# Two expert stages rewritten in a chain of sixteen layers: choice in one pass, gathering in units, combination on 32-column parts

## The reference

```python
def _L3_ffn_ref(x, Wc, bc, W1, b1, W2, b2):
    DM, NEXPERTS, SETS, ESIZE = (128, 32, 4, 32)
    grouped = x.reshape(b, s // g, g, d)                       # g = 32 tokens
    logits = jnp.einsum('bntd,des->bntes', grouped, Wc) + bc
    tie = jnp.linspace(0.0, 1e-06, g, dtype=x.dtype).reshape(-1, 1, 1)
    logits = logits + tie
    perm = (logits == jnp.max(logits, axis=-3, keepdims=True)).astype(x.dtype)
    permuted = jnp.einsum('bntd,bntes->bnesd', grouped, perm)
    inner = jax.nn.relu(jnp.einsum('bnesd,esdf->bnesf', permuted, W1) + b1)
    result_permuted = jnp.einsum('bnesf,esdf->bnesd', inner, W2) + b2
    result = jnp.einsum('bnesd,bntes->bntd', result_permuted, perm)
    return result.reshape(b, s, d)
...
x = x + _L3_ffn_ref(_layernorm(x, axis=-1), ...)
```

## Time and profile before

| | before |
|---|---|
| time, median of 2 runs | 2715.27 us (2713.83 to 2716.72) |
| the profiled execution's own time | 2716.01 us |
| its span, first to last instruction | 2714.2 us |
| mean granted TensorE clock | 0.894 |
| TensorE busy | 2225.2 us (82%) |
| VectorE busy | 1772.0 us (65%) |
| ScalarE busy | 1385.8 us (51%) |
| first expert stage | 2302.0 to 2398.6 us |
| second expert stage | 2607.9 to 2705.6 us |

### The profile page before, as it was taken

One profiled execution on the slowest core, in us unless ns is written; L12 is line 12 of the kernel. 1 busy time (PEld: TensorE's weight loads), 2 busy tenths in 40 slices (PEclk: granted clock), 3 DMA queues, 4 the chain that ended last, 5 costly groups with the idle time before them and its releaser, 6 DMA issues. The chain is left out here.

```text
span 2714.2 us, 42839 instructions
## 1 busy us (share of the span) xinstructions
PE 2225.2 (82%) x15196; PEld 1524.2 (56%) x15196; DVE 1772.0 (65%) x4423; ACT 1385.8 (51%) x3630; POOL 718.8 (26%) x472
## 2 busy tenths in 40 slices
PE   6999979889887987978447887768776988689978
PEld 4888846636643653653347774433424765556648
DVE  6777748759746965964656663356456997637863
ACT  3555537738734764864411226563636764326750
POOL 0000016516502642630033420000012976051000
PEclk9999999989988989999678898888987999778986
DMA  1000021100002101001012320000001221100010
GB/s 56 14 19 15 7 72 22 23 20 21 21 5 75 25 17 24 21 16 48 0 36 58 74 46 0 12 12 6 4 12 56 86 70 60 45 10 2 2 65 17
DMA packets 79043, 80.92 MB, mean 30 GB/s; under 512 B 28624, under 2 KB 63952, under 8 KB 77808
## 3 DMA queue, kind: packets, MB, share of 16 engines
q1 hardware_dynamic: 78832, 78.19, 10.1%
HBM read 53.94 MB, written 8.52 MB: 23 GB/s over the span
## 5 line engine op out<-in xcount | busy, mean ns | idle before, releaser
L1014 ACT ACTIVATE window_s<-window_s,window_soft 128x128 f32<-128x128 f32 x512 | 197.7, 394 | 5.0 <-DVE window_soft L1177 5.0
L1084 POOL TENSOR_TENSOR window_s<-window_s,window_soft 128x512 f32<-128x512 f32 x128 | 133.2, 1041 | 218.5 <-DVE window_soft L1114 218.4
L1092 POOL TENSOR_TENSOR window_pa<-window_pa,window_pb 128x1024 f32<-128x1024 f32 x64 | 151.5, 2368 | 148.8 <-DVE window_pb L1159 148.8
L1177 DVE CUSTOM_DVE_ANT_0 window_s<-ps,window_mask,window_nrn 128x128 f32<-128x128 f32 x512 | 148.7, 346 | 46.7 <-PE ps L859 29.9
L3127 DVE TENSOR_TENSOR_SCAN mamba_bx<-ps,mamba_ab 128x256 f32<-128x256 f32 x256 | 154.5, 667 | 18.9 <-PE ps L2913 18.9
L822 PE MATMUL ps<-window_wa,window_sh 128*128 128x512 f32 x256 | 131.3, 638 | 41.4 <-DVE window_pb L1159 28.4
L3297 ACT ACTIVATE rope_p<-ps,rope_mx 128x128 f32<-128x128 f32 (+1 forms) x256 | 104.3, 419 | 53.1 <-DVE rope_mx L3351 53.1
L2910 PE MATMUL ps<-mamba_m,mamba_xt 128*128 128x129 f32 x512 | 102.9, 283 | 29.6 <-ACT mamba_m L2985 20.6
L83 PE MATMUL ps<-x,consts 128*128 128x512 f32 x120 | 77.0, 801 | 46.1 <-PEq L53 40.5
L3015 POOL TENSOR_TENSOR h<-mamba_bx,mamba_cbr 128x1024 f32<-128x1024 f32 x32 | 89.3, 2796 | 93.2 <-DVE mamba_bx L3127 92.7
L2910 PEld LDWEIGHTS ps<-mamba_m,mamba_xt 128*128 128x128 f32 x512 | 82.3, 197 | 49.1 <-issue 49.1
(11 more groups left out here) (607 smaller groups left out, 6235.9 us busy)
## 6 DMA issues: line engine op xcount, KB each, us to landing
mamba_cbr<-mamba_c SPq DMA_DIRECT2D x32, 512.0 KB, 3.7
window_vs<-window_vt SPq DMA_DIRECT2D x64, 128.0 KB, 2.3
delta_xi<-delta_x SPq DMA_DIRECT2D x16, 512.0 KB, 5.1
switch_w<-in_switch_w SPq DMA_DIRECT2D x4, 2048.0 KB, 10.1
window_wa<-in_window_wa SPq DMA_DIRECT2D x4, 1152.0 KB, 6.8
linattn_wb<-in_linattn_wb SPq DMA_DIRECT2D x6, 513.0 KB, 3.5
window_wb<-in_window_wb SPq DMA_DIRECT2D x4, 537.5 KB, 7.7
window_sh<-y SPq DMA_DIRECT2D x16, 128.0 KB, 2.2
```

The lines of the kernel that those rows point to most:

```text
L1014: a = nc.scalar.activation(s[:, k % 2, e, c, :], s[:, k % 2, e, c, :], ACT.Exp, scale=-1.0, bias=soft[:, k % 2, e, 1, c:c + 1], accum_out= ...
L1084: nc.gpsimd.tensor_tensor(s[:, k % 2, e], s[:, k % 2, e], soft[:, k % 2, e, 3, :].unsqueeze(2).to_broadcast([P, QC, P]), ALU.mult)\
L1092: nc.gpsimd.tensor_tensor(own, own, pb[:, :, :, :].rearrange("p a h d -> p (a h d)"), ALU.add)\
L1177: v = nc.vector.tensor_tensor_reduce(s[:, k % 2, e, c, :], K.ps[:, B_S + e, toks(c, P)], mask[:, k % 2, :], nrn[:, k % 4, h:h + 1], 3e38, ...
```

## The change

Only `switch_stage` changes, in five places.

1. Choice in one pass: VectorE adds bias and tie term in one scalar_tensor_tensor straight from PSUM, in place of ScalarE's pass and VectorE's add.
2. Order: the logits of a block and the turning of its tokens alternate on TensorE. The turning of `perm` and the gathering start as soon as two blocks are chosen. VectorE copies a first gathered half block before it makes the fourth choice. ScalarE makes all copies of turned `perm`.
3. Gathering in units: a unit (j, u) is eight matmuls, for the four tiles of block j and for two of the four groups. The groups go to banks j and j + 4; ScalarE copies the one, VectorE the other, and neither waits for the other's copy. `z` is laid out as [feature, group, expert], so the copies write runs of 128 elements, and the first product reads its 64 moving elements 128 elements (512 bytes) apart.
4. The results are turned without b2; copies alternate between ScalarE and VectorE. b2 comes in through matmuls of `perm` (as stationary operand, 128 experts by 128 tokens) with b2.
5. Combination: for each group `perm`'s 32 columns are the stationary operand and `resm[:, group, :]` the moving one, with the output on 32 partitions, so four groups go to four 32-column parts of the array. The sum has tokens on the partitions; ScalarE copies it to `y_tm`, TensorE turns it back, and VectorE adds it to `x`.

```diff
-    z = st.sb("z", [P, ES, NG])
+    z = st.sb("z", [P, NG, ES])
...
+    units = [(0, 0), (1, 0), (0, 1), (2, 0), (1, 1), (3, 0), (2, 1), (3, 1)]
+    seen = {u: n + 1 for n, u in enumerate(units)}
+
+    def picked_to(j, g):
+        return z[:, :, :].rearrange("p (j t g) e -> p j g t e", j=NJ, g=4)[:, j, g]
...
+            def turn_chosen(j):
                 pe.wait_ge(st.chosen, j + 1)
+                pe.wait_ge(st.x_copied, j + 1)
                 for t in range(TPW):
                     mm = nc.tensor.transpose(K.ps[:, j, toks(t, P)], perm[:, toks(TPW * j + t, P)], K.ident)
                 mm.then_inc(st.chosen_tm, 1)
...
+            def pick(j, u):
+                pe.wait_ge(st.chosen_copied, j + 1)
+                if u:
+                    pe.wait_ge(st.picked_act, seen[j, 0])
+                    pe.wait_ge(st.picked_dve, seen[j, 0])
+                for t in range(TPW):
+                    for e in range(2):
+                        g = 2 * u + e
+                        rows, tile = slice(32 * g, 32 * g + 32), toks(TPW * j + t, P)
+                        mm = nc.tensor.matmul(K.ps[:, j + 4 * e, toks(t, P)], h_tm[rows, tile], perm_tm[rows, tile],
+                                              start=True, stop=True)
+                mm.then_inc(st.picked, 1)
...
+            def combine(j):
+                bank = K.ps[:, 4 + j % 2, :]
                 if j >= 2:
+                    pe.wait_ge(st.y_copied, j - 1)
+                for t in range(TPW):
+                    nc.tensor.matmul(bank[:, toks(t, P)], perm[:, toks(TPW * j + t, P)], b2, start=(t == 0), stop=False,
+                                     skip_group_check=True)
+                pe.wait_ge(st.moved_act, 2 * (j + 1))
+                pe.wait_ge(st.moved_dve, 2 * (j + 1))
                 for t in range(TPW):
                     for g in range(4):
+                        n = 4 * (TPW * j + t) + g
+                        mm = nc.tensor.matmul(K.ps[32 * g:32 * g + 32, 4 + j % 2, toks(t, P)], perm[:, toks(n, GT)],
+                                              resm[:, n, :], start=False, stop=True, skip_group_check=True)
+                mm.then_inc(st.y_ready, 1)
...
                     mm = nc.tensor.matmul(K.ps[32 * r:32 * r + 32, q // 8, toks(q % 8, NG)], w1[:, 4 * q + r, :],
-                                          z[:, 4 * q + r, :], start=True, stop=True)
+                                          z[:, :, 4 * q + r], start=True, stop=True)
...
-                nc.scalar.activation(logit[:, toks(j)], K.ps[:, j, :], ACT.Identity, bias=bc).then_inc(st.biased, 1)
...
+                nc.vector.scalar_tensor_tensor(grouped(logit[:, toks(j)]), grouped(K.ps[:, 4 + j, :]), bc,
+                                               tie.unsqueeze(1).to_broadcast([P, 16, GT]), ALU.add, ALU.add)\
+                    .then_inc(st.logits, 1)
...
+            choose(0)
+            choose(1)
+            choose(2)
+            picked(*units[0])
+            choose(3)
+            for j, u in units[1:]:
+                picked(j, u)
```

More of the change, by code:

```diff
@@ L3472, in _, with turn_back @@
+            def turn_back(j):
+                pe.wait_ge(st.y_copied, j + 1)
+                if j >= 2:
+                    pe.wait_ge(st.x_done, j - 1)
+                for t in range(TPW):
+                    mm = nc.tensor.transpose(K.ps[:, 6 + j % 2, toks(t, P)], y_tm[:, toks(TPW * j + t, P)], K.ident)
+                mm.then_inc(st.y_turned, 1)
             outer.pe(pe, 0, K.x, lambda j: None)
@@ L3474, in _ @@
             for j in range(NJ):
[L3475 to L3497, removed]
+                logits(j)
+                turn_x(j)
+            turn_chosen(0)
+            turn_chosen(1)
+            for n, (j, u) in enumerate(units):
+                pick(j, u)
+                if n in (1, 3):
+                    turn_chosen(2 + n // 2)
             pe.wait_ge(st.w2_ready, 32)
-            pe.wait_ge(st.picked_copied, NT)
+            pe.wait_ge(st.picked_act, 8)
+            pe.wait_ge(st.picked_dve, 8)
             for q in range(NQ):
@@ L3516, in _ @@
                             mm.then_inc(st.h2_ready, 1)
[L3517 to L3524, removed]
-            for j in range(NJ):
-                pe.wait_ge(st.result_ready, min(4 * j + 4 + 8, NT))
-                for g in range(16 * j, 16 * j + 16):
-                    mm = nc.tensor.matmul(K.ps[:, 4 + j, toks(g % 16, GT)], resm[:, g, :], perm[:, toks(g, GT)],
-                                          start=True, stop=True)
-                mm.then_inc(st.y_ready, 1)
+            turn_result(0)
@@ L3544, in _ @@
-            for n in range(0, NT, 2):
-                picked_copy(scalar_copy, act, n)
-            for n in range(0, ES // 8, 2):
-                result_copy(scalar_copy, act, n)
+                nc.scalar.activation(h_tm[:, toks(j)], K.ps[:, j, :], ACT.Copy).then_inc(st.x_copied, 1)
+            turned_chosen(0)
+            turned_chosen(1)
+            for n, (j, u) in enumerate(units):
+                picked(j, u)
+                if n in (1, 3):
+                    turned_chosen(2 + n // 2)
@@ new lines, in _ @@
+            for n in range(0, ES // 8, 2):
+                act.wait_ge(st.h2_ready, n + 1)
+                if n:
+                    act.wait_ge(st.h2_copied, n)
+                nc.scalar.activation(result_to(n), K.ps[:, (4 + n) % 8, :].rearrange("p (q g) -> p q g", g=NG), ACT.Copy)\
+                    .then_inc(st.h2_copied, 1)
+            moved(0)
+            moved(2)
+            for j in range(NJ):
+                if j + 1 < NJ:
+                    moved(4 * j + 4)
+                    moved(4 * j + 6)
+                result(j)
```

132 lines of the change are left out of this document (80 added, 52 removed).

## The result

The changed kernel takes 2669.27 us (median of 2 runs, 2667.62 and 2670.93) against 2715.27 before: a ratio of 0.983, 95% interval 0.981 to 0.986. Run again beside others it took 2666.7 us (five runs, 2662.1 to 2670.2), ratio 0.982 (0.980 to 0.983). Forecast were 2664 us, with 2646 to 2692 as range.

The account below looks back on a forecast made before the run. TensorE was busiest at 82% of the span, but the two stages' four parts had different limits. Gains of 2 x (11.6 + 12.9) + 3.0 = 52.0 us off 2716.0 gave 2664.0 us, range 2646 to 2692.

Parts of the forecast that it names:

- Gathering: Choice and gathering, each stage: 27.8 us for 39.45, a gain of 11.6 (9.1 to 14.1, by clock level).
- First product: First expert product, moving operand now read 512 bytes apart: a cost of 0 to 1 us.
- rival 1: First product: strided reads queue at one reader, 0.58 us a round, +12.8 us a stage, 2690 us in all; chance 0.22.
- Second product: Second expert product: its sixteen copies keep their strict turns, so no change from 14.18 and 13.72 us.
- Turning and combination: Last part of each stage: 22.7 us for 35.6, a gain of 12.9, with the clock high after the start.
- changes of mode: Last part: eight more TensorE changes between whole-array and tiled matmuls, 0.8 to 1.6 us, 1.5 taken.
- the tail: Last part, after the last round: signals, ScalarE copy and VectorE add, 2.2 us with gaps.
- Behind the stages: Next stage's centring (2.2 us) and the store's turnings (about 0.8) gain 3.0 us if the stages end high.
- The clock staying low: Both stages stay at 1.2 GHz: gains 9.1 + 2.6 a stage, nothing behind, 2693 us; chance 0.11.
- The clock staying high: Clock high throughout: gains 14.1 + 15 and about 3 in the products a stage, 3 behind, 2649 us; chance 0.13.
- Slower: First product: queued reads at 1.98 ns an element, 1.01 us a round, +26.5 us a stage, 2717 us; chance 0.04.
- Units that change nothing: Gathering: copies take turns on PSUM after all, 1.2 us a unit, about 2 us a stage lost, inside the range.

Follow-up runs that it names:

- by fours: Changed kernel with z laid out [feature, four, group, expert in the four], so copies write runs of 16 bytes; 2659.6 us (0.980).
- pairs: Changed kernel with z by pairs of experts, elements read 8 bytes apart, and the second product's copies without turns; 2651.7 us (0.977).
- the old layout: Changed kernel with z again expert before group: copies write 256 bytes apart, first product reads side by side; 2660.7 us (0.979).

## Why the prediction was right or wrong, point by point

- **Sum and sign: right in direction, 52.0 forecast, 46.0 by the medians and 48.4 by the spans.** One term failed, the first product, which lost 9.4 us and stood in the sum with nothing. The others gave 5.8 us more than forecast: combination 2.1, gathering 1.5, second product 1.2, outside the stages 1.0. That they made up for more than half of the miss is luck; the sum came out closer than its parts.
- **Gathering, 11.6 a stage (9.1 to 14.1): 10.1 and 14.6, mean 12.3.** The bounds are the two levels of the clock, and the two stages stand near either: 0.78 and 0.94. Ends were forecast at 25.3 or 30.3 us, and 26.6 and 29.4 came. The first stage beat its low end because four units took 6.07 us for 6.8: units on different row groups overlapped, and their starts came 1.0 to 1.5 us apart. The second missed its high end because its centring, at 1.2 GHz, took 1.7 us more; by fours, without that, gathering took 24.9. The sum set 27.8 against the first stage's 39.45 for both, but the second took 41.16 before, so 1.7 us of its gain were left out. The scalar_tensor_tensor took 0.74 us (0.75 forecast), a unit 0.9 to 1.0 us at the high level. Contiguous copies on VectorE take 0.69 us; the 0.62, a quarter of a row of four, is the distance at which they start when they stand back to back (1.88 us for three).
- **First product, "0 to 1": wrong. It cost 4.6 and 4.8 us a stage.** This is the step that failed: "I take 0 to 1, since the contiguous rounds already draw 512 elements in 0.11 us". How fast side by side elements come says nothing of elements far apart. And the row taken as the nearest, the turning of strided results, spaces the operand that is loaded as weights (`res[:, :, g]` against the identity; the rows name the streaming operand first, here `consts`), not the one that streams; its 1.1 ns an element is no price of a moving read, at either level of the clock. Neither of the two prices for a strided round, 0.15 us if each part reads for itself and 0.58 if they take turns, is what a round takes: 0.29, and 0.37 in the first rounds. The four parts together read 1.8 elements per ns, for 4.6 side by side. No run has one part reading alone, so whether they share a reader stays open. The time fell into the range all the same, because the range was wide enough for rival 1 and the other terms gave more.
- **Second product, no change: 0.8 and 0.4 us shorter.** The sixteen copies by turns took 12.55 us in either stage after the change, and 12.54 and 12.97 before. In the first stage the whole gain is that their first began 0.7 us behind the last maximum and not 1.6.
- **Turning and combination, 12.9 a stage: 14.0 and 13.9.** Rounds of four at 0.22, bias matmuls at 0.22 and a high clock (0.93 and 0.92) came as forecast. The 1.5 us for changes of mode was somewhat too much: from the first turning to the end of the last combining round 19.5 us passed, for 18.5 summed (19.0 without the last block's turning back), so about 1.0 lies in changes and slower turnings; the tail, with that last turning back, took 2.1 for 2.7. The Trainium skill (TensorEngine Tiling (Array Packing), Key Properties) says that a change of tiling mode drains TensorE; here the next block's first turning began 0.20 us behind the start of the last combining matmul, where turnings follow each other by 0.15, and no run isolates the drain.
- **Behind the stages, 3.0: 3.8.** Between the stages 3.3, of which the centring gave 2.25 (5.92 to 3.67), and 0.5 behind the second, for 0.8.
- **Rivals.** Queued strided reads: the effect is there at a third of its price, 4.7 us a stage for 12.8. The clock staying low: in the first stage's gathering (0.78), not at the end. The clock staying high: for the end of the stages and for the second stage's gathering behind its normalization. Slower: no, a round took 0.29 to 0.38 us and not 1.0. Units that change nothing: no, both engines copied at the same instant, and taking turns cost 1.8 and 5.5 us.

## What to carry to other kernels

A layout has a writer and a reader, and both prices count: moving a stride of z from sixteen copies to 128 matmuls shortened each copy by a third or more and made the product nearly twice as long (5.9 to 10.7 us). A layout between the two served both better: with runs of 16 bytes the copies kept their full speed and the product took 7.7 us. Semaphores that make two engines take turns can look like mere bookkeeping; taking them out of the second product gave 11.4 us, more than either other layout of z. And what a shorter step wins can be lost in the next one: with pairs the second product ran at half clock in the one profile taken, and with the old layout it grew by 1.7 to 1.9 us a stage. Look at the time and the granted clock of the part behind, not only at the part that was shortened.

## What the runs showed of the hardware that I had not expected

- Strided moving reads by four 32-column parts at 2.4 GHz: 0.112, 0.118, 0.236, 0.284 and 0.29 us a round of 4 x 64 fp32 elements, read twice, at 4, 8, 16, 256 and 512 bytes. At 1.2 GHz: 0.213 at 4 and 8 bytes, 0.236 at 16. The first third at 512 bytes takes 0.37 at either level.
- While they ran, VectorE was slower too: the first addition of the bias took 1.03 us in the first stage and 1.15 in the second, for 0.69 otherwise, and the maximum behind it 0.62 and 0.73, for 0.43. TensorE's rounds took 0.31 to 0.36 us at that moment, on their way from 0.37 to 0.29. The later additions took 0.69 to 0.74 beside rounds of 0.29. Why the first third of the product is slower than the rest is open.
- Two engines that both write 256 bytes apart take 1.29 and 1.25 us a copy on average in the first stage, where most of their copies start together, and mostly 1.04 in the second, where they overlap but start 0.2 us apart or more; by turns they took 1.03 and 1.01.
- 235 records of the second product (29 rounds) took 12.3 us, 0.42 us a round, with the clock at 0.50 for all but the first 0.9 us and TensorE busy all along; at 1.00, 220 records took 6.1 us, 0.22 a round. Being busy did not bring the clock back there, as it did not under the old combination (17.2 us at 0.51).
